# Two-layer attention and expert kernel: moving the loads of the attention stacks in SyncE's queue

## The reference

```
xn = layernorm(x)
q = xn @ wq (32 heads of 8), k, v = xn @ wk, xn @ wv (8 heads of 8, each shared by 4 query heads)
s = softmax(q k^T / sqrt(8), causal) v @ wo
f = sum over the 4 best of 32 experts of weight * (u * silu(g)) @ down,  g, u = xn @ gate_up
x = x + s * silu(f)
```

## Time and profile before

| | |
|---|---|
| median of 3 executions | 1968.14 us (1967.16 to 1971.93) |
| the profiled execution | 1972.94 us, span of the core 1971.2 us |
| busy over the span | PE 91%, DVE 72%, ACT 50%, POOL 36% |
| granted TensorE clock, mean | 0.969 of full |

### The profile page before, as it was taken

One profiled execution on the slowest core, in us unless ns is written; L12 is line 12 of the kernel. 1 busy time (PEld: TensorE's weight loads), 2 busy tenths in 40 slices (PEclk: granted clock), 3 DMA queues, 4 the chain that ended last, 5 costly groups with the idle time before them and its releaser, 6 DMA issues.

```text
span 1971.2 us, 43826 instructions
## 1 busy us (share of the span) xinstructions
PE 1789.6 (91%) x14838; PEld 1289.3 (65%) x14838; DVE 1418.7 (72%) x2477; ACT 990.6 (50%) x2744; POOL 704.7 (36%) x870
## 2 busy tenths in 40 slices
PE   5567888788879999999999999999999999999997
PEld 3226765233355567787777877877877877778776
DVE  4776785011167658888888888888888888888887
ACT  1002223677712235665565665665656655656654
POOL 5640001111040041552642634625615526436344
PEclk9679998899979999999999999999999999999999
DMA  6625674000012220001001001001010010010010
GB/s 250 217 79 162 195 198 130 23 21 22 0 59 65 90 73 18 33 11 43 32 11 43 32 11 43 14 29 43 0 43 32 11 43 32 11 43 32 11 54 21
DMA packets 76372, 112.40 MB, mean 57 GB/s; under 512 B 24332, under 2 KB 57756, under 8 KB 73122
## 3 DMA queue, kind: packets, MB, share of 16 engines
q1 hardware_dynamic: 72810, 102.95, 15.9%
q0 software_dynamic: 3072, 8.39, 1.4%
q10 hardware_dynamic: 446, 0.48, 0.1%
HBM read 86.22 MB, written 28.73 MB: 58 GB/s over the span
## 4 chain that ended last, share of the span: by engine, by line
PE 50%; ACT 9%; DVE 5%; issue 5%; POOL 1%; DMA 0%; ACTq 0%; DVEq 0%; SPq 0%; POOLq 0%
PE ps L1324 9%; PE ps L1371 6%; PE ps L1381 4%; PE ps L1515 3%; PE ps L1618 3%; PE ps L1605 3%; PE ps L1620 3%; ACT gmask_Q L1760 2%; PE ps L1589 2%; PE ps L1594 2%; PE ps L1555 2%; PE ps L1398 2%; PE ps L1408 2%; PE ps L1425 2%; PE ps L1346 2%
## 5 line engine op out<-in xcount | busy, mean ns | idle before, releaser
L1840 POOL TENSOR_TENSOR kq_decayed<-conv,decay_rows 128x256 f32<-128x256 f32 x234 | 181.6, 800 | 459.3 <-PE ps L1618 459.3
L1969 DVE SCALAR_TENSOR_TENSOR conv<-raw,tap_st,conv 128x1024 f32<-128x1024 f32 x202 | 280.8, 1390 | 3.6
L1324 PE MATMUL ps<-xnT,w_conv_st 128*128 128x512 f32 x544 | 248.3, 600 | 0.2 <-issue 0.2
L817 DVE TENSOR_REDUCE m_part<-ps 128x1 f32<-128x640 f32 (+7 forms) x176 | 175.9, 1027 | 70.0 <-PE ps L668 44.7
L999 ACT ACTIVATE probs<-ps 128x1024 f32<-128x1024 f32 (+7 forms) x256 | 146.0, 660 | 58.0 <-PE ps L934 28.7
L1324 PEld LDWEIGHTS ps<-xnT,w_conv_st 128*128 128x128 f32 x544 | 99.0, 192 | 101.4 <-issue 97.0
L1381 PE MATMUL ps<-w_z_st,xnT 128*128 128x256 f32 x512 | 150.4, 396 | 0.0
L904 POOL DMA_INDIRECT slot_outputs<-scratch_slots_y,token_slots x32 | 30.6, 956 | 318.5 <-POOLq L497 209.6
L1639 ACT COPY raw<-ps 128x512 f32<-128x512 f32 x136 | 80.7, 593 | 125.8 <-PE ps L1324 125.0
L645 PE MATMUL ps<-k_stack,q_stack 128*128 128x512 bf16 (+3 forms) x384 | 100.8, 355 | 39.7 <-DVE m_part L817 22.8
L1026 DVE COPY oT<-ps 128x1024 f32<-128x1024 f32 x8 | 9.8, 1225 | 171.6 <-PE ps L921 171.6
(11 more groups left out here) (356 smaller groups left out, 4336.6 us busy)
## 6 DMA issues: line engine op xcount, KB each, us to landing
decay_rows<-scratch_egc SPq DMA_DIRECT2D x17, 1024.0 KB, 4.8
w_conv_st<-in_w_conv SPq DMA_DIRECT2D x17, 512.0 KB, 3.3
scratch_slots_x<-yacc SPq DMA_DIRECT2D x8, 1024.0 KB, 14.8
slot_rows<-scratch_slots_x SPq DMA_DIRECT2D x16, 512.0 KB, 4.8
scratch_slots_y<-slot_outputs SPq DMA_DIRECT2D x16, 512.0 KB, 3.5
w_gate_up<-in_gu SPq DMA_DIRECT2D x8, 768.0 KB
w_gate_up<-in_gu SPq DMA_DIRECT2D x32, 192.0 KB
k_nat_decayed<-in_gu SPq DMA_DIRECT2D x22, 256.0 KB, 2.8
```

The source lines that it names most:

```text
L817: dve.tensor_reduce(dst, src, AX.X, ALU.max).then_inc(s_max, 1)
L1324: mm = pe.matmul(ps[:, 6 + n % 2, :], wc[:, k, (n // 2) * P:(n // 2 + 1) * P], m.xnT[:, k, (n % 2) * HALF:(n % 2 + 1) * HALF], start=k == ...
L1840: op = g.tensor_tensor(kqe[:, e, :, at], cv[:, 0:2, at], egr[:, e, at].unsqueeze(1).broadcast_to([P, 2, P]), ALU.mult)
L1969: op = dve.scalar_tensor_tensor(out=cv[:, t, :], in0=raw[:, t, at:at + T], scalar=tap[:, t, at:at + 1], in1=cv[:, t, :], op0=ALU.mult, op1 ...
```

## The change

Only SP's queue in the stage of maxima and experts is rewritten. No transfer is added or removed; their order and the waits between them change.

| | before | after |
|---|---|---|
| stack 1 | at the start of the stage | the same |
| stack 2 | right behind stack 1 | behind stack 1, once 16 score operations are made |
| stack 3 | behind the weights of steps 0 and 1 | behind stack 2, once 30 are made |
| weights of steps 0 and 1 | behind stack 2 | behind stack 3 |
| stack 4 | before the wait for the scatter and the rows of steps 0 and 1 | behind these rows |
| stacks 5 and 6 | behind the rows of steps 0 and 1, once 23 and 45 score operations are made | 5 behind the store in turn g = 2, 6 behind that in turn g = 4 |
| stack 7 | behind the store in turn g = 2 | behind the store in turn g = 6 |

```diff
             load_stacks(sp, m, 1)
+            sp.wait_ge(s_sc, 16)
             load_stacks(sp, m, 2)
+            sp.wait_ge(s_sc, 30)
+            load_stacks(sp, m, 3)
             sp.wait_ge(m.s_rows, 16 * (E0 // G0))
             for g in range(2):
                 load_weights(g, g)
-            load_stacks(sp, m, 3)
-            sp.wait_ge(s_sc, 1)
-            load_stacks(sp, m, 4)
             sp.wait_ge(s_scat, 16 * NC * TOP0)
             for g in range(2):
                 load_rows(g, g)
-            for group in range(5, NKV - 1):
-                sp.wait_ge(s_sc, (group - 4) * GROUP_OPS + 1)
-                load_stacks(sp, m, group)
+            load_stacks(sp, m, 4)
             for g in range(2, STEPS // 2):
                 sp.wait_ge(s_t, turn_count(g - 2, 1) + 1)
                 load_rows(g, g % 2)
                 sp.wait_ge(s_gu, 2 * (g - 2) + 2)
                 load_weights(g, g % 2)
                 sp.wait_ge(s_yc, 2 * (g - 2) + 2)
                 store_outputs(g - 2, g % 2)
-                if g == 2:
-                    sp.wait_ge(s_sc, (NKV - 5) * GROUP_OPS + 1)
-                    load_stacks(sp, m, NKV - 1)
+                if g % 2 == 0:
+                    group = 4 + g // 2
+                    sp.wait_ge(s_sc, (group - 4) * GROUP_OPS + 1)
+                    load_stacks(sp, m, group)
```

## The result

| | before | after |
|---|---|---|
| median | 1969.18 us (10 executions) | 1976.26 us (10 executions, 1970.08 to 1981.75) |
| ratio of the times, 95% interval | | 1.0035 (1.0020 to 1.0049) |
| profiled execution, span | 1972.94, 1971.2 us | 1976.45, 1974.7 us |

What follows compares the result with a forecast made beforehand. PE, busy for 91% of the span, was taken as the bound. Front 0, rows 2 x 5.1 = 10.2 and clock 2 x 2.4 = 4.8 gave +15.0 on 1968.1, so 1983.1 us; 8 in 10 range 1974 to 1989 us.

Steps and rivals of the forecast that it cites:

- The front's term: Score operations up to `turn(0, 0)` at 137.87 us: moved stacks and weights gain 0, bounds 0 and 17.5 us.
- the back's terms: Expert steps after 137.87 us: two new waits for rows, 10.2 us, plus low clock behind them, 4.8 us.
- three stops of equal length: DVE idle 8.9 us up to 82.8 us and 8.6 up to 112.3; ACT 8.8 from 342.2; put to POOL's bursts.
- The second stop: DVE's loss of 8.6 us up to 112.3 us, at 27% DMA with no stack or weight; evidence against transfers.
- The waits for rows, 2 x 5.1: Steps 5 and 7: rows issued 4.2 us later behind a stack, landing in 7.0; PE waits 5.1 us each.
- The clock behind each wait, 2 x 2.4: After the late turns of steps 5 and 7, PE's clock falls to 1.2 GHz, costing 2.4 us each.
- The rival in which the clock holds: Steps 5 and 7: waits come without the clock falling, or half of each; +10.2 to 12.6 us, chance 0.16.
- so this wait stays: 0: Step 3: stack 5 replaces stack 7 ahead of the rows, so PE's 6.04 us wait is unchanged.
- So the two waits and the moves cost nothing: Front: SP's new waits for 16 and 30 score operations and the moved transfers delay nothing PE needs; cost 0.
- the one case of 6.04 us: PE's wait for step 3's rows behind stack 7 before the change; model for the new waits and clock loss.
- the one on the other side: Front: transfers cause DVE's stops; both go, net -2.5 us, or only the first, +6.1 us; chance 0.12 in all.
- The fast landing: Steps 5 and 7: rows land fast, waits 1.8 us each, no clock fall; +3.6 us, 1971.7 us, chance 0.10.

Runs made afterwards that it cites:

- e4: Kernel before with POOL's 32 scatters in bursts of 8 instead of 16, a stack clearing behind every eighth; 1955.45 us, ratio 0.9921.
- e9: Kernel before with all 32 scatters of POOL in one burst and all clearing of stacks behind it; 1976.14 us, ratio 1.0028.
- e5: Changed kernel with the wait ahead of stack 2 at 22 score operations instead of 16; 1981.25 us, ratio 1.0057.
- e6: Changed kernel's front, stacks 5 to 7 moved behind the gate and up weights, POOL's scatters in bursts of 8; 1949.52 us, ratio 0.9892 to before.
- e11: Changed kernel unaltered, run again on the chip without stops; 1945.10 us, ratio 1.0056 to the kernel before.
- e2: Kernel before with its old front, only stacks 5, 6, 7 moved behind the stores of turns 2, 4, 6; 1979.94 us, ratio 1.0059.

## Why the prediction was wrong

The prediction said +15.0 us, and +7.1 us was measured. The 7.9 us between them come from two of its terms. The front's term was wrong in its mechanism and is worth 3.0 us; the back's terms were right in kind and place, and too large by 3 to 5 us.

- *The front's gain, where the prediction says "so I take a gain of 0, with bounds of 0 and 8.9 + 8.6 = 17.5 us": this is the step that failed.* It was argued from three stops of equal length at different DMA shares that the transfers have no part in them. They have a smaller one: with the 2.3 MB of weights beside the first burst, DVE's stop (the first gap of over 0.7 us once it is going) begins 9.8 to 12.1 us behind the first score operation, and without them 13.3 to 15.0 us behind it, which is worth 3.0 us by the lengths of the front. The first half of the argument held (the bursts make the stops: e4, e9, and e5 for what remains without transfers). The wrong inference was from "not the main cause" to "no effect". The second stop, which had looked the cleanest evidence, indeed does not depend on the bulk: 8.6 us at a share of 0.27, 9.5 us at 0.94.
- *The waits for rows, 2 x 5.1: right in kind and place, mis-sized.* They measured 4.62 and 4.22 in the changed kernel, and 4.4 in the mean over the five profiles with both. SP was late by 4.1 us, where 4.2 were foreseen; the landing was 6.8 and 6.2 us instead of the 7.0 taken from a single case.
- *The clock behind each wait, 2 x 2.4: it fell both times, also mis-sized.* From `turn(5, 0)` to the second up product it is 197.75 - 192.34 = 5.41 us against 199.20 - 195.52 = 3.68 before, and from `turn(7, 0)` 225.61 - 220.17 = 5.44 us against 3.73, so 1.7 us each. The rival in which the clock holds is out. The products, the first two after the change and the last before it:

```profile
197.75 1.07 PE L697 MATMUL ps<-slot_rows_turned,w_gate_up 128*96 128x128 f32 x8
225.61 1.06 PE L697 MATMUL ps<-slot_rows_turned,w_gate_up 128*96 128x128 f32 x8
...
199.20 1.06 PE L698 MATMUL ps<-slot_rows_turned,w_gate_up 128*96 128x128 f32 x8
```

- *"so this wait stays: 0" for step 3.* In the profile it is 1.9 us shorter, and the 1.58 us wait behind it is gone. Over the profiles it is 3.9 to 6.7 us, mean 5.2, where step 3 alone has a stack, and 3.5 to 4.9 us, mean 4.1, where steps 5 and 7 have one too. The two sets overlap; whether the change shortens this wait by 1 us or single executions scatter is not shown.
- *"So the two waits and the moves cost nothing":* right; PE waited for no stack in any of these kernels.

The sum with the measured terms is -3.0 + 2 x (4.4 + 1.7) = +9.2 us, against +7.1 measured, within its interval of 3.9 to 9.6. The lengths of the back give less than the terms: in the mean 193.3 us over the five profiles with a stack at step 3 alone (191.8 to 194.5) and 203.7 us over the five with all three (201.0 to 207.4), so +10.4 us for the two waits. With that the sum is -3.0 + 10.4 = +7.4 us. The prediction had 15.0 for this part, so its sizes, taken from the one case of 6.04 us, make the larger share of the difference.

The measured 1976.3 us lies within the range of 1974 to 1989 us, but not for the reason that was given. Of the rivals, the one on the other side comes nearest in number (1974 us, if only the first stop goes); it was right about a part of its mechanism (the first stop has to do with transfers) and wrong about the size, for the stop became 3 us shorter and did not go. The fast landing is refuted. On the chip without stops the front's term is 0 as I had it, and +10.8 us came out, where the back's terms, as measured, make 12.2 and its lengths 10.4.

## What to carry to other kernels

In a queue that serves several consumers, look at how late the load behind the insertion point may come, not at how early the inserted one is needed: here the same nine issues cost 5 to 7 us each in front of the rows and nothing that shows in the time that the queue would have waited anyway. A term that the trace bounds by 0 and 17.5 us should not be set to 0 because the main cause lies elsewhere. When a profile shows an engine idle with its inputs long there, vary the neighbour that is busy at the time (here the length of POOL's bursts) before anything else: that one was worth twice the whole change.

## What the runs showed of the hardware

- From the eighth to the twelfth indirect DMA of an unbroken series of POOL on, DVE starts its instructions up to 6.6 us late although their inputs are there (e9, at 94.69), until 1 to 5 us behind the last of the series. ACT does the same from the seventh of the gathers on (8.9 to 9.2 us, also "remote"). With breaks of 4.5 us behind every eighth no idle time of DVE in the front was put down to "remote" any more (e4, e6); its idle time in the front fell from 22 us to 7.3 and 3.6 us. What delays the start I could not settle. The Trainium skill (SBUF — State Buffer, "Who interferes with whom") rules out the shared port for tensor_reduce; the runs agree in so far as ACT is struck too, and no run shows what it is instead.
- It was there in all 13 profiles of the other chips (with bursts of 8 only in ACT, under the gathers) and in none of the 3 of one chip, where the kernel before takes 1934 us in place of 1969. The bursts themselves run at the same pace on both, a scatter every 1.27 us.
- A wait of PE of 4.22 us was enough for a granted clock of 1.2 GHz behind it, and so was one of 3.54 us (e11, step 3) and, after score operations that each waited for DVE, one of 2.13 us (e6). The length of the wait alone doesn't decide: behind 3.84 us (e2, step 3) the clock stayed at 2.4 GHz. The windows are those of e11 and e2:

```profile
146.40:149.00 2.60, 2.56 (x12) 2.17 (x13) 0.67 (x1) 0.58 (x1) 0.00 (x0) 0.50 0.18 76
...
165.90:168.70 2.80, 2.71 (x21) 2.38 (x22) 1.31 (x2) 0.58 (x1) 0.00 (x0) 1.00 0.32 134
```
